# Second layer of a two-layer attention and expert kernel: key, value and query loads moved from ScalarE's queue to the sync queue behind each turn's row of maxima, with a fifth key stack and a smaller heads tensor

## The reference, cut to what matters

```python
q = split_heads(queries @ Wq.T)          # 16 heads of 16
k = split_heads(keys @ Wk.T)
v = split_heads(values @ Wv.T)
scores = jnp.einsum('bhqd,bhkd->bhqk', q, k) * scale
attn = jax.nn.softmax(scores, axis=-1)
ctx = jnp.einsum('bhqk,bhkd->bhqd', attn, v)
out = ctx.transpose(0, 2, 1, 3).reshape(queries.shape[0], -1, D)
return out @ Wo.T
```

## Time and profile before

| | |
|---|---|
| median of 3 runs (909.52 to 912.53) | 910.83 us |
| the profiled execution's own time | 915.3 us |
| its span, first to last instruction | 913.6 us |
| mean granted TensorE clock, share of full speed | 0.953 |
| TensorE matmul busy | 798.5 us, 87% |
| VectorE busy | 474.5 us, 52% |
| ScalarE busy | 263.3 us, 29% |
| GpSimd busy | 278.3 us, 30% |
| first instruction of turn 0 | 664.01 us |
| first instruction of turn 15 | 881.64 us |

### The profile page before, as it was taken

One profiled execution on the slowest core, in us unless ns is written; L12 is line 12 of the kernel. 1 busy time (PEld: TensorE's weight loads), 2 busy tenths in 40 slices (PEclk: granted clock), 3 DMA queues, 4 the chain that ended last, 5 costly groups with the idle time before them and its releaser, 6 DMA issues. The chain is left out here.

```text
span 913.6 us, 14282 instructions
## 1 busy us (share of the span) xinstructions
PE 798.5 (87%) x5120; PEld 523.5 (57%) x5120; DVE 474.5 (52%) x1100; ACT 263.3 (29%) x522; POOL 278.3 (30%) x295
## 2 busy tenths in 40 slices
PE   5987999799989799899999999897588788689985
PEld 4664567465755464555666565455465466456663
DVE  2447473247444667143445545266267766576722
ACT  1223211321141122022222322122145543345550
POOL 4564314131400506105315263268422211000011
PEclk8999999999999999999999999899779998899998
DMA  7787734332520857436866557659747963945100
GB/s 211 206 261 224 205 90 154 103 98 66 152 75 1 293 209 240 131 116 188 212 182 184 159 165 188 157 158 197 148 104 149 149 158 89 160 87 108 19 22 21
DMA packets 70206, 133.34 MB, mean 146 GB/s; under 512 B 9989, under 2 KB 50950, under 8 KB 68218
## 3 DMA queue, kind: packets, MB, share of 16 engines
q1 hardware_dynamic: 54312, 81.02, 29.4%
q10 hardware_dynamic: 7986, 31.16, 17.3%
q0 software_dynamic: 7840, 20.26, 8.4%
HBM read 103.92 MB, written 28.31 MB: 145 GB/s over the span
## 5 line engine op out<-in xcount | busy, mean ns | idle before, releaser
L1561 DVE TENSOR_REDUCE mxh<-ps 112x2 f32<-112x750 f32 x128 | 115.2, 932 | 57.4 <-PE ps L1861 57.4
L1272 PE MATMUL ps<-rw,rowsT 128*128 x280 | 132.8, 618 | 1.5 <-ACT rowsT L1233 0.8
L1733 ACT ACTIVATE d_pT<-ps 125x448 f32<-125x448 f32 x192 | 90.6, 548 | 86.9 <-PE ps L1881 86.7
L988 PE MATMUL ps<-x1T,sw 128*128 128x448 f32 x256 | 102.8, 547 | 6.1 <-DVE gluT L459 4.6
L1272 PEld LDWEIGHTS ps<-rw,rowsT 128*128 128x128 f32 x280 | 51.9, 195 | 60.1 <-issue 60.1
L988 PEld LDWEIGHTS ps<-x1T,sw 128*128 128x128 f32 x256 | 46.8, 190 | 51.7 <-issue 38.2
L1861 PE MATMUL ps<-kst,qst 96*112 96x375 bf16 x256 | 66.0, 351 | 8.7 <-DVE mxh L1561 4.4
L1881 PE MATMUL ps<-qst,kst 128*128 128x112 bf16 x768 | 54.2, 225 | 18.0 <-DMA qst<-mT 10.5
L1289 PE MATMUL ps<-rw,gT 128*128 x280 | 66.4, 380 | 0.8 <-ACT gT L1237 0.8
L1289 PEld LDWEIGHTS ps<-rw,gT 128*128 128x128 f32 x280 | 52.9, 190 | 21.4 <-issue 16.0
L1881 PEld LDWEIGHTS ps<-qst,kst 128*128 128x128 bf16 x768 | 46.0, 105 | 28.9 <-DMA qst<-mT 11.5
(11 more groups left out here) (222 smaller groups left out, 1290.3 us busy)
## 6 DMA issues: line engine op xcount, KB each, us to landing
rb<-in_rb SPq DMA_DIRECT2D x35, 512.0 KB, 4.2
rw<-in_rw SPq DMA_DIRECT2D x24, 512.0 KB, 10.3
kscr<-ka SPq DMA_DIRECT2D x16, 567.0 KB, 3.5
kst<-kscr ACTq DMA_DIRECT2D x15, 567.0 KB, 6.3
cT<-in_ctx_t SPq DMA_DIRECT2D x21, 378.0 KB, 9.6
ctxT<-in_ctx_t SPq DMA_DIRECT2D x16, 378.0 KB
ctxn<-in_ctx SPq DMA_DIRECT2D x16, 375.0 KB
kst<-kscr ACTq DMA_DIRECT2D x15, 378.0 KB, 7.7
```

The lines of the kernel that those rows point to most:

```text
L988: last = mm(bank[up_in(i, m)[k]][:, 0:GS], w[:, e, c, h * P:(h + 1) * P], x1T[:, c, :], start=c == 0, stop=c == C - 1)
L1272: last = mm(bank[1 + 2 * q + k], rowsT[:, q, c * P:(c + 1) * P], w[:, e, c, :], start=c == 0, stop=c == C - 1)
L1561: V.tensor_reduce(mxh[:, 2 * g:2 * g + 2], ps[0:S, 2 * (g % 2):2 * (g % 2) + 2, 0:K], axis=AX_X, op=ALU.max).then_inc(s["s_max"], 1)
L1733: A(pT[:, q % 2, k, :], bank[4 + k][0:KC, 0:QUAD * S], ACT.Exp).then_inc(s["p_ready"], 1)
```

## The change

All loads of the loop leave ScalarE. Sync issues, in turn b and in this order: the maxima of b + 1 (as before), the values of b + 1, the keys of b + 4, and in the first two turns of groups 1 and 2 three of the six query loads of the next group. Before, all six went out in the first turn of the group. A fifth key stack lets the keys of b + 4 be loaded before turn b has finished with its own; GpSimd fills its lower rows with ones once. `heads` keeps two groups in place of all sixteen batches, which makes the room. VectorE waits for the experts' last tile before its first maximum.

```diff
+    STACKS = 5
-    kst, qst, cT = (kst_0, kst_1, kst_2, kst_3), (qst_0, qst_1), (cT_1, cT_0, cT_2)
+    kst, qst, cT = (kst_0, kst_1, kst_2, kst_3, kst_4), (qst_0, qst_1), (cT_1, cT_0, cT_2)
...
     def load_key_copies(eng, b, part):
         first_copy, n = ((0, 3), (3, 2), (5, 1))[part]
-        eng.dma_start(kst[b % 4][first_copy * HD:(first_copy + n) * HD, :, :].rearrange("p h t -> p (h t)"),
-                      kscr[b].rearrange("s (d g) x -> (s d) (g x)", d=HD)[0:n * HD, :]).then_inc(s[f"k_in{b % 4}"], 16)
+        eng.dma_start(kst[b % STACKS][first_copy * HD:(first_copy + n) * HD, :, :].rearrange("p h t -> p (h t)"),
+                      kscr[b].rearrange("s (d g) x -> (s d) (g x)", d=HD)[0:n * HD, :]).then_inc(s[f"k_in{b % STACKS}"], 16)
...
             if b + 1 < B:
                 maxima(b + 1)
+
+            if b and b + 1 < NV:
+                sp.wait_ge(s["pv_ps"], b)
+                load_values(b + 1)
+            if b + 4 < B:
+                if b:
+                    sp.wait_ge(s["st_ps"], b * 4 * NKC)
+                load_keys(sp, b + 4)
+            if i in (1, 2) and j < 2:
+                sp.wait_ge(s["st_ps"], i * G * 4 * NKC)
+                load_queries(sp, i + 1, range(3 * j, 3 * j + 3))
             if j == 3 and i:
                 results(i - 1)
...
         pool.wait_ge(s["va_ready"], 2)
+        ones_below(pool, 4)
...
+        v.wait_ge(routed["y_ready"], NTILE)
         for g in range(8):
             maximum(0, g)
...
             if b:
                 keep_outputs(b - 1)
-                if b + 1 < NV:
-                    load_values(b + 1)
...
             exps(b, 1)
-            if b in (G, 2 * G):
-
-                load_queries(a, b // G + 1)
             exps(b, 2)
...
             exps(b, 3)
-            if b + 4 < B:
-                load_keys(a, b + 4)
...
-            if b < 4:
+            if b < STACKS:
                 t.wait_ge(s["ones_ready"], b + 1)
```

More of the change, by code:

```diff
@@ L1314, in second_layer @@
     QUAD = 4
+    STACKS = 5
     yscr, kscr, vscr, qscr = (dram[n] for n in ("yscr", "kscr", "vscr", "qscr"))
-    ((cT_1, cT_2, kst_1, vt, qst_1, kst_2, kst_3, va, pT, outT, heads, res, mxh, mr, mparts, mT, rec),
+    ((cT_1, cT_2, kst_1, vt, qst_1, kst_2, kst_3, kst_4, va, pT, outT, heads, res, mxh, mr, mparts, mT, rec),
      (wq1, wo1, wf, vrT, cfT, bf_b, identb, stat, mv, rstd, yg, xh, xhT, qa, qr, kst_0, qst_0, wv1, cT_0)) = tensors
-    kst, qst, cT = (kst_0, kst_1, kst_2, kst_3), (qst_0, qst_1), (cT_1, cT_0, cT_2)
+    kst, qst, cT = (kst_0, kst_1, kst_2, kst_3, kst_4), (qst_0, qst_1), (cT_1, cT_0, cT_2)
     s = {n: new_semaphore("d_" + n) for n in (
@@ L1322, in second_layer @@
         "q_ps", "q1_ready", "q2_ready", "q3_ready", "q_out", "qs_in0", "qs_in1",
-        "k_in0", "k_in1", "k_in2", "k_in3", "v_in0", "v_in1", "s_ps", "s_max", "m_ready", "mT_ps", "mT_ready", "clear", "ones_ready",
+        "k_in0", "k_in1", "k_in2", "k_in3", "k_in4", "v_in0", "v_in1", "s_ps", "s_max", "m_ready", "mT_ps", "mT_ready", "clear", "ones_ready",
         "mrow_in0", "mrow_in1", "st_ps", "p_ready", "pv_ps", "outT_ready", "out_ps", "heads_ready", "o_ps", "x3_ready", "bf_added",
@@ L1587, in finish @@
             v.wait_ge(s["heads_ready"], b * 2 + 1)
-            V.tensor_tensor(heads[:, b, :].rearrange("p (h d) -> p h d", d=HD), out_ps[:, :, 0:HD],
+            V.tensor_tensor(heads[:, b % (2 * G), :].rearrange("p (h d) -> p h d", d=HD), out_ps[:, :, 0:HD],
                             rec[:].unsqueeze(2).to_broadcast([S, NH, HD]), ALU.mult).then_inc(s["heads_ready"], 1)
@@ L1669, in store_queries, with load_queries @@
         a.dma_start(qscr[i].rearrange("s p x -> p s x"), qa[:].rearrange("p s c t -> p s (c t)")).then_inc(s["q_out"], 16)
[L1671 to L1675, removed]
+    def load_queries(eng, i, copies=range(6)):
+        eng.wait_ge(s["q_out"], (i + 1) * 16)
+        for r in copies:
+            k = (0, 0, 0, 1, 1, 2)[r]
+            eng.dma_start(qst[i % 2][r * HD:(r + 1) * HD, :, :].rearrange("p h t -> p (h t)"),
+                          qscr[i, k].rearrange("(d g) x -> d (g x)", d=HD)).then_inc(s[f"qs_in{i % 2}"], 16)
     def scalar_beside(a, m):
@@ L1737, in keep_outputs @@
             A(outT[:].rearrange("p q t -> p (q t)"), bank[7][:, 0:GS], ACT.Copy).then_inc(s["outT_ready"], 1)
-        def load_values(b):
-            a.dma_start(vt[:, b % 2, :, :, :].rearrange("p c h d -> p (c h d)"), vscr[b]).then_inc(s[f"v_in{b % 2}"], 16)
         for c in range(C):
@@ L1860, in scores @@
                 h = 2 * g + k
-                last = mm(bank[2 * (g % 2) + k][0:S, 0:K], qst[i % 2][0:DEPTH, h, j * S:(j + 1) * S], kst[b % 4][0:DEPTH, h, 0:K], start=True, stop=True)
+                last = mm(bank[2 * (g % 2) + k][0:S, 0:K], qst[i % 2][0:DEPTH, h, j * S:(j + 1) * S], kst[b % STACKS][0:DEPTH, h, 0:K], start=True, stop=True)
             last.then_inc(s["s_ps"], 1)
@@ L1869, in arrived @@
         def arrived(b):
-            t.wait_ge(s[f"k_in{b % 4}"], (b // 4 + 1) * 3 * 16)
+            t.wait_ge(s[f"k_in{b % STACKS}"], (b // STACKS + 1) * 3 * 16)
             semaphore, value = queries_in(b)
@@ L1880, in transposed @@
                 for h in range(QUAD):
-                    last = mm(bank[4 + k][:, h * S:(h + 1) * S], kst[b % 4][:, QUAD * q + h, k * KC:k * KC + P],
+                    last = mm(bank[4 + k][:, h * S:(h + 1) * S], kst[b % STACKS][:, QUAD * q + h, k * KC:k * KC + P],
                               qst[i % 2][:, QUAD * q + h, j * S:(j + 1) * S], start=True, stop=True)
@@ L1991, in tensor @@
                     t.wait_ge(s["xh_ready"], (NORMS[what, i] + 1) * G)
-                turn_over(heads[:, i * G:(i + 1) * G, :] if what == "o" else xh)
+                turn_over(heads[:, i % 2 * G:(i % 2 + 1) * G, :] if what == "o" else xh)
             transposed(b, 3)
@@ L2017, in tensor @@
         t.wait_ge(s["heads_ready"], B * 2)
-        turn_over(heads[:, (NG - 1) * G:NG * G, :])
+        turn_over(heads[:, (NG - 1) % 2 * G:((NG - 1) % 2 + 1) * G, :])
         project("o", NG - 1, wo1, "o_ps")
@@ L2063, in build_program @@
                 ("qst_1", [P, NH, GS], BF16), ("kst_2", [P, NH, KP], BF16), ("kst_3", [P, NH, KP], BF16),
-                ("d_va", [KC, B - NV, NKC, NH, HD + 1], F32),
+                ("kst_4", [P, NH, KP], BF16), ("d_va", [KC, B - NV, NKC, NH, HD + 1], F32),
                 ("d_pT", [KC, 2, NKC, GS], F32), ("outT", [P, 4, S], F32),
-                ("heads", [S, B, D], F32), ("res", [S, G, D], F32), ("mxh", [S, NH], F32), ("mr", [S, 2, NH], F32),
+                ("heads", [S, 2 * G, D], F32), ("res", [S, G, D], F32), ("mxh", [S, NH], F32), ("mr", [S, 2, NH], F32),
                 ("mparts", [S, 2, 3, NH], BF16), ("mT", [3 * NH, 2, S], BF16), ("rec", [S, NH], F32)))
```

## The result

The changed kernel takes 947.67 us (947.05 to 951.05, 4 runs) against 911.68 us for the kernel before beside it: 3.8% slower, ratio 1.0377 with a 95% interval of 1.0341 to 1.0414. The prediction had the side right, but 923.5 us and a range up to 936.

A forecast was written before the change was run, and what follows sets the result against it. TensorE (busy 87%) and, in short turns, the DMA engines were taken as near their limit. -14.85 + 15 (values) + 9 (queries) + 3.5 (clock) = +12.65 on 915.3 gave 928, less 4.5: 923.5 us, range 905 to 936.

The forecast's parts named there:

- what goes: Waits on maxima at turns 4, 5, 9 and on values at turn 2 vanish: 12.85 us, 14.85 with the clock.
- which waits come, and where: Turns 2, 3, 4, 8, 9 wait for values, +15 us; turns 6 and 10 for queries, +9 us.
- I take 7.6 us, near the second, because the keys are behind and not ahead: Landing time of values against 4.65 us left: five turns start 3.0 us late each, +15 us.
- The bounds, 7.2 and 11.1: Upper limits on the values' landing, in us, read from the loads that turns 3 and 2 needed.
- The row that I rejected as too crowded: Turn 2's values, with key loads ahead and gathers beside, landed in 11.1 us or less; 7.6 was taken.
- the queries: Second half of the query loads arrives late in turns 6 and 10: 6 and 3 us, together +9.
- The step from 186 GB/s: Turn 5's 2945 kB at that rate take 15.8 us against 10.3 available: 5.5 too long, taken as 6.
- I charge 0.5 us each: Clock cost of seven stalls of 3 to 6 us in place of two long ones: +3.5 us.
- the 2.0 that it took off for old ones: Matmuls at the lower clock after the stalls ahead of turns 5 and 9: 0.5 + 1.5 us removed.
- the difference carries over: The profiled execution of the kernel before lies 4.5 us above the median; so 928 becomes 923.5 us.
- The third rival, "one after another": Values take 11.1 us and queries their upper bounds: +45, 956 us; chance 0.12, most between 933 and 945.
- the estimate of 4.8 us: Values landing on five engines by the skill's figures: five turns lose 0.2 us each, 1 us in place of 15.

The follow-up runs named there:

- values_back: The changed kernel with only the values back on ScalarE's queue, early in the turn: 915.62 us, ratio 1.0024 to the kernel before.
- values_first: The changed kernel with the values in one DMA on sync's queue but ahead of the turn's maxima: 918.76 us, ratio 1.0002 to the kernel before.
- values_split: The changed kernel with each load of values cut into two DMAs of 112 and 13 partitions: 908.52 us, ratio 0.9931 to the kernel before.
- queries_whole: The changed kernel with all six query loads in turns 4 and 8, behind the keys: 945.06 us, ratio 1.0223 to the kernel before.
- keys_back: The changed kernel with only the keys back on ScalarE's queue at the turn's end: 935.53 us, ratio 1.025 to the kernel before.
- split_queries: The kernel before with values loads cut into 112 and 13 partitions and six query loads behind the maxima on sync's queue: 902.82 us, ratio 0.9884.

## Why the prediction was right and wrong

**Right: what goes.** The 12.85 us of waits at turns 2, 4, 5 and 9 that the prediction counted as removed: no turn start in the changed kernel waits for the maxima. (Turn 2's wait was for values and came back as 2.60. The 12 us until turn 5 were misread, it is 13.1; nothing hangs on it.)

**Right: which waits come, and where.** Five short turns wait for values, turns 6 and 10 for the queries' second half, and nothing waits at 5, 7, 11 or later. values_back, values_first and values_split each take the first group away; queries_whole takes away the second.

**Wrong: "I take 7.6 us, near the second, because the keys are behind and not ahead".** The values took 9.2 to 9.7 us with keys behind, 11.0 with gathers too. Keys behind are not harmless; keys_back shows that sending them 2 us later already takes 2 us off. The term is 23.6 us, not 15. The bounds, 7.2 and 11.1, held. The prediction said that no row times the values alone; the DMA share of the kernel before does, 5.9 us at most, so 7.6 had room for less than 2 us of company. The row that I rejected as too crowded was the nearer one.

**A little low: the queries.** 7.11 and 5.19 us against 6 and 3: 12.3 for 9. The step from 186 GB/s was good for turn 6.

**Wrong: "I charge 0.5 us each".** This is the largest miss. Beyond the waits themselves the turns grew by 11.8 us, where the prediction had 3.5 for new stalls less the 2.0 that it took off for old ones, so 1.5. I had taken 0.5 us from turn 5 after a stall of 2.93 us, though the same rows gave 1.5 for turn 9 after one of 6.87. Now turns 2, 3 and 4 run at 0.81, 0.80 and 0.74 of the clock, and turn 4 alone, with no stall in it, needs 3 us more: its clock fell twice. The clock does come back to 1.00 between the stalls, and not every turn pays: turn 3 is no longer than before. values_back shows the size from the other side: waits of 17.8 us went, and some 12 us with them. How much of the 11.8 us is the clock alone was not separated. Turn 1 grew by 2.9 us with a clock of 0.88, and in it VectorE and ScalarE both stood still until 680.1 for a cause that the profile doesn't name.

**Wrong: "the difference carries over".** The prediction took 4.5 us off because the profiled execution of the kernel before lay above its median. The changed kernel's profiled execution, 947.05, lies 0.6 below its own, so 5.1 us were missing that no mechanism explains.

Together: 8.6 for the values, 3.3 for the queries, 10.3 for the turns, 5.1 for the executions, less 3.0 outside the loop, are 24.3 us, where 923.5 to 947.67 is 24.2. No one term put the time out of the range: with the turns' growth right it would have been 937, still above 936.

 The third rival, "one after another", had the mechanism that won, loads that crowd each other, with its 11.1 us for the values; its chance of 0.12 and its cut back to 933 to 945 were too low.

**The rule that was weighed.** The Trainium skill's rule on 125 partitions bore on the case, and I used it the wrong way round. I let the estimate of 4.8 us speak for values in time. The load that ran on a third of the engines (0.34) was one that company slowed from 5.9 us to over 9, and one that could be mended in a line; that was the larger finding.

## What to carry to other kernels

A load that is issued later in the period than before needs its landing time among its new neighbours, not alone; take the most crowded row as the likeliest, not as the bound. When TensorE waits for a DMA, read the DMA share between that load's issue and its landing, not over the turn. A stretch at a third of the engines says to look at the shape of the load before its place: here cutting 125 partitions into 112 and 13 moved the ratio from 1.038 to 0.993 in one order and from 1 to 0.983 in the other, loads ahead of the loop included. Stalls that recur each turn can cost more than their length, since here each was followed by matmuls at the lower clock; take that cost from the longest stall that the rows show, not from the shortest.

## What the runs showed of the hardware

A small DMA on its own queue is not insulated: in the kernel before three rows of 3.5 KB, issued 1 us behind query loads on the other queue, were still missing 13 us later, and putting only the query loads behind them (split_queries) took one wait of 2.43 us away and brought one of 8.65 us down to 2.47. A load of 398 KB over 125 partitions took 5.9 us at most nearly by itself, with a third of the DMA engines busy, 7.2 to 7.9 with 1134 KB of keys issued 2 us later on the other queue, 9.2 to 9.7 with the keys directly behind it, and 4.6 and 5.5 us cut in two with the same keys behind it. The granted clock fell to its lower level (0.50, 1.2 GHz) in or right behind waits of 2.6 to 5.9 us ahead of turns 2, 3 and 4, and was back at 1.00 (2.4 GHz) in between; the means of these turns were 0.81, 0.80 and 0.74. In turn 4 it fell a second time with no wait over 1.15 us in front of it, and that turn took 3 us more than before.
